# A graph attention layer on one core: the second half of the one-hots turned at the first tile of a group

## The reference

```python
def head(w1, bb1, w2, bb2, a1, aab1, a2, aab2):
    feats = jnp.maximum(x @ w1 + bb1, 0.0) @ w2 + bb2
    x_cat = jnp.concatenate([feats[row], feats[col], elem[:, None]], axis=1)
    hid = jnp.maximum(x_cat @ a1 + aab1, 0.0)
    e1 = (hid @ a2 + aab2)[:, 0]
    e1 = jax.nn.leaky_relu(e1, negative_slope=0.2)
    w = jnp.exp(e1 - jnp.max(e1))
    pooled = jax.ops.segment_sum(w[:, None] * feats[col], row, num_segments=n)
    row_sum = jax.ops.segment_sum(w, row, num_segments=n) + 1e-10
    return pooled / row_sum[:, None]
...
x = _layernorm(x + _L0_gnn_ref(x, edge_index, edge_weight, ...), axis=-1)
```

## Time and profile before

| | us |
|---|---|
| median of 3 timed runs | 5230.21 (5229.04 to 5233.76) |
| the profiled execution | 5190.44 |
| its span, first to last instruction | 5188.7 |
| tile loop | about 1700 to 4960 |
| busy, share of the span | PE 85%, DVE 88%, ACT 72%, POOL 52% |
| granted TensorE clock, mean | 0.956 |

### The profile page before, as it was taken

How to read it: one execution, slowest core, us unless ns; L and a number is a source line. 1 busy time by engine, 2 the same in 40 slices (tenths; PEclk the granted TensorE clock), 3 DMA queues, 4 the chain that set the end, 5 groups by cost and what they waited for, 6 DMA issues and landing times.

```text
span 5188.7 us, 133139 instructions
## 1 busy us (share of the span) xinstructions
PE 4402.2 (85%) x24914; PEld 3093.9 (60%) x24915; DVE 4550.7 (88%) x25629; ACT 3761.1 (72%) x12720; POOL 2702.7 (52%) x2834
## 2 busy tenths in 40 slices
PE   1499899999986899999999999999999999999920
PEld 0255555555554666767677767767677767767610
DVE  7799999999998789888899889889898889898853
ACT  0467766766762688888888888888888888888832
POOL 1266666666666555555555555555555555555522
PEclk9799999999997999999999999999999999999965
DMA  2032333333333777777777777777777777777623
GB/s 79 23 73 67 78 72 71 75 74 72 69 78 93 227 216 218 218 219 217 216 218 217 217 218 219 217 218 216 217 218 216 219 215 219 215 220 216 200 87 117
DMA packets 287022, 850.50 MB, mean 164 GB/s; under 512 B 98946, under 2 KB 138114, under 8 KB 286966
## 3 DMA queue, kind: packets, MB, share of 16 engines
q0 software_dynamic: 169920, 673.54, 46.8%
q1 hardware_dynamic: 74638, 160.14, 9.7%
q10 hardware_dynamic: 42408, 16.21, 1.2%
HBM read 738.46 MB, written 111.26 MB: 164 GB/s over the span
## 4 chain that ended last, share of the span: by engine, by line
PE 29%; ACT 25%; DVE 6%; issue 4%; DMA 4%; DVEq 1%; POOL 0%; ACTq 0%; POOLq 0%; SPq 0%
ACT z L1092 17%; PE psum L949 12%; PE psum L953 7%; PE psum L936 6%; DVE z L1503 3%; ACT onehot L1121 3%; DMA out_dram<-z 3%; ACT onehot_t L1110 3%; PE psum L962 2%; ACT onehot L1125 2%; PE psum L973 1%; DVE z L1493 1%; PE psum L921 1%; DVE acc L1552 1%; DVEq L1552 0%
## 5 line engine op out<-in xcount | busy, mean ns | idle before, releaser
L734 POOL DMA_INDIRECT z<-qf_table,rec x1664 | 1593.6, 958 | 1567.0 <-PE psum L936 1035.8
L1092 ACT ACTIVATE z<-z 128x64 f32<-128x64 f32 x6656 | 1651.5, 336 | 56.6 <-ACT z L1099 56.3
L949 PE MATMUL psum<-p_win,onehot_t 128*128 x9984 | 1434.0, 276 | 207.7 <-ACT onehot_t L1110 90.5
L949 PEld LDWEIGHTS psum<-p_win,onehot_t 128*128 128x128 bf16 x9984 | 963.9, 97 | 777.8 <-issue 460.6
L936 PE MATMUL psum<-z,onehot 128*128 128x260 f32 x3328 | 1027.2, 391 | 2.8 <-DVE acc L1552 1.9
L953 PE MATMUL psum<-z,ident 128*128 128x258 f32 x3328 | 1004.0, 383 | 0.0
L1503 DVE SCALAR_TENSOR_TENSOR z<-z,a_b 128x129 f32<-128x129 f32 x3328 | 893.0, 292 | 0.0
L1503 DVE SCALAR_TENSOR_TENSOR z<-psum,a_b 128x129 f32<-128x129 f32 x3328 | 822.6, 283 | 0.0
L1552 DVE TENSOR_TENSOR acc<-acc,psum 125x260 f32 x1664 | 698.7, 420 | 78.6 <-PE psum L936 48.8
L1493 DVE TENSOR_TENSOR z<-z,psum 128x258 f32<-128x258 f32 x1664 | 691.9, 416 | 39.4 <-PE psum L953 29.6
L666 POOL DMA_INDIRECT sorted_rows<-z x300 | 483.3, 1611 | 406.9 <-DVE z L1384 162.4
(11 more groups left out here) (221 smaller groups left out, 6363.0 us busy)
## 6 DMA issues: line engine op xcount, KB each, us to landing
p_table<-acc SPq DMA_DIRECT2D x100, 377.9 KB
p_win<-p_table SPq DMA_DIRECT2D x100, 377.9 KB
qf_table<-acc SPq DMA_DIRECT2D x75, 378.9 KB
z<-qf_table,rec POOLq DMA_INDIRECT x1664, 4.6
acc<-in_x_dram SPq DMA_DIRECT2D x25, 500.0 KB
z<-in_x_dram SPq DMA_DIRECT2D x20, 625.0 KB
out_dram<-z ACTq DMA_DIRECT2D x20, 625.0 KB
qf_table<-z SPq DMA_DIRECT2D x25, 378.9 KB
```

The source lines that it names most:

```text
L734: pool.indirect_dma_start(out=z_t[:, o + j, :], out_offset=None, in_=qf_table, in_offset=bass.IndirectOffsetOnAxis(ap=rec[:, o + j, 3:4].b ...
L949: mm = pe.matmul(to, onehot_t[:, j, :], p_flat[:, bass.ds((w % 2) * (3 * ZW) + (part * ZW + o), n)], start=(part == 0), stop=(part == 2 an ...
L1092: op = act.activation(z_t[:, slot, o:o + DO], z_t[:, slot, o:o + DO], ACT.Copy, scale=z_t[:, slot, o + DO:o + HF])
```

## The change

The turn of the second half of a group's one-hots moves on TensorE from behind the third `hidden_src` to behind the first. The copy of this half on ScalarE moves from the head of the group's own step to the step before, between the weights of the sixth and the seventh tile. Nothing is computed otherwise.

```diff
                 for j in range(SB):
                     if live(i, k, 0):
                         hidden_src(j)
-                    if j == SB // 4 and live(i, k, 0):
+                    if j == 0 and live(i, k, 0):
                         turn(0, 1)
                     if j == SB // 4 and live(i, k, -1):
                         max_t()
...
-                if live(i, k, 0):
-                    take_turned(0, 1)
                 if live(i, k, 1):
                     onehots(1, 0)
                 if live(i, k, -1):
...
                     if j == SB // 2 and live(i, k, 1):
                         onehots(1, 1)
+                    if j == SB - 3 and live(i, k, 1):
+                        take_turned(1, 1)
```

## The result

The changed kernel took 6033.2 us (median of 4 runs, 6031.1 to 6048.4) beside 5230.3 for the kernel before: 1.154 times as long, 95% interval 1.152 to 1.156. The forecast was 6231 us with a range of 5570 to 6330. The profiled execution took 6033.65 us, 843 more than that of before.

The account below looks back on a forecast made before the run. VectorE was taken to bound the loop; 17.33 us per group plus 3.1 for the clock gave 20.43 against 15.57, over 206 groups 1001 us, plus 5190.4 profiled and 39.8 offset: 6231 us, range 5570 to 6330.

Parts of the forecast that it names:

- part 1: TensorE, at the moved turn: it waits 2.3 to 3.0 us per group for the second half's one-hots.
- parts 2 and 3: VectorE's delay behind the turn and the closed cycle: 8.19 + 2.38 + 6.70, corrected to 17.33 us per group against 15.57.
- T: End of ScalarE's Relu for the second half's one-hots, put at 8.19 us after `e_sh`.
- part 5: TensorE's clock in the loop: the stall halves it in nearly every group, costing 3.1 us each.
- rival B: Clock in the loop: falls for only 3.4 us or in some groups; 5881 us, mixtures 5700 to 6100; chance 0.22.
- main case: Whole loop: stall plus 6.8 us at half clock, 20.43 us per group; 6231 us (6130 to 6330); chance 0.43.
- the sort's row: Trace of the sort: clock fell inside a TensorE pause, 6.8 us at half; taken as model for the loop.
- the tail: Trace's end: after a 1.73 us pause and smaller ones the clock fell for 3.4 us, TensorE working from its start.
- VectorE bounds the loop, and the copy's wait is worth 0.3 us at most: Tile loop before: VectorE limits it; removing all its waits for TensorE would bring 0.2 to 0.3 us per group.
- part 4: ScalarE's moved copy: waits for nothing, own time neither saved nor added; `onehots(1, 0)` starts at about T + 5.9.
- D: Moved turn: its one-hots are ready when it is reached; 5168 us at best, 5230 without gain; chance 0.07.
- A: Loop: only the stall costs, clock stays at 2.4 GHz; 5593 us (5525 to 5670); chance 0.22.

Follow-up runs that it names:

- turn_only: The kernel before with only TensorE's turn moved to behind the first hidden_src, the copy left in place: 6022.7 us, 1.160 times before.
- oh_third: The changed kernel with ScalarE's onehots(1, 1) moved from behind the fifth weight to behind the third: 5271.2 us, 1.008 times before.
- oh_second: The changed kernel with ScalarE's onehots(1, 1) moved from behind the fifth weight to behind the second: 5145.3 us, 0.984 times before.
- fill8: The changed kernel with 8 needless f32 products on constants on TensorE ahead of the turn: 5609.2 us, 1.073 times before.
- copy_only: The changed kernel with the turn back behind the third hidden_src, so only ScalarE's copy moves: 5045.8 us, 0.9725 times before.
- extra_before: The kernel before with two needless small copies on ScalarE ahead of the second half's copy at the step's head: 5248.9 us, 1.0116 times before.
- turn_at_1: The changed kernel with the turn behind the second hidden_src instead of the first: 5252.7 us, 1.012 times before.
- split_dve: copy_only with the second of VectorE's two register loads moved from the group's start to ahead of the fourth tile: 5048.8 us, 0.9729 times before.

## Why the prediction was right, and where it was off

*The stall* (part 1): forecast 2.3 to 3.0 us ahead of the turn, measured 2.84. *Right*, forecast from the trace of before alone; `turn_only` shows that it needs nothing else, `oh_third` and `oh_second` that it hangs on the time of the one-hots and not on the place as such.

*The cycle* (parts 2 and 3): forecast 17.33 us a group at full clock, measured 17.35 to 17.47 in the groups without a fall and 17.41 as a typical value in `fill8`. The terms hold too, by the medians of the eight groups without a fall: from T to the second tile forecast 2.38, measured 2.41; from there to `e_sh` forecast 6.70, measured 6.75. ScalarE's part, forecast 8.19, measured 8.25 in the group shown. *Right.*

*The clock falls* (part 5): forecast in nearly every group. The clock fell in 165 of 173 groups. *Right*, and `fill8` shows that idleness of TensorE is what brings it: with 1.0 us of pause on average the clock fell in 2 of 136 groups. The length of the pause alone doesn't decide: eight groups with the full pause of 2.4 to 3.1 us had no fall, and `oh_third` has falls at shorter ones. The page of the Trainium skill named in the prediction (TensorE: Matmul & The Clock Gate, HAM oscillation) would have it stay up here; the trace does not agree.

*What the fall costs*: this is the term that was mis-sized. I put 3.1 us on every group, for 6.8 us at the low level, and gave the short fall (3.4 us, a loss of 1.4) as rival B. Both occur, half and half. In the long groups T to the exponentials took 12.06 us (3503.36 to 3515.42), where the sum has 9.1 without a fall, a loss of 2.9. In the short ones it took 10.5 where the clock fell inside the stall, a loss of 1.4, and 10.9 where it fell behind it, 1.7. The groups take 20.2 to 20.4 and 18.7 to 19.2 us, where main case and B have 20.43 and 18.73. The two prices were about right and the share was wrong: 2.15 us on average instead of 3.1. My reason for taking the sort's row was that the low level would begin inside the pause. It began behind the pause in 42 of the 165 falls, as in the tail, and in 43 more it began inside and was short all the same. By its own ranges the forecast's main case (6130 to 6330) missed; 6033 us lies in rival B's mixtures (5700 to 6100), and the stated range holds it because it was drawn wide enough to take in both. That the two lengths came out even is nothing that the prediction knew, and why a fall takes one or the other is open beyond the times named above.

*Medians*: I added 39.8 us because the timed runs of before lay that much above its profile. The changed kernel's median is that of its profile (6033.2 and 6033.7). The difference of the profiles, 843 us, is 158 less than my 1001, that of the medians 198; the offset should have gone into the range. Of the 158, the groups account for more than all, 206 x (20.43 - 19.56) = 179 us; the rest of the kernel came out 21 us longer than in the profile of before, and 179 - 21 + 40 are the 198. Most of that lies ahead of the loop: the first exponentials start at 1752 us against 1728, and so they do, within 6 us, in all four runs on the chip where before takes 5230 us. They start at 1728 in `turn_only`, so it isn't the edit.

*VectorE bounds the loop, and the copy's wait is worth 0.3 us at most*: *wrong*, though it changed nothing in the result. I read it from the list of waits, where VectorE's for TensorE came to 0.21 us. `copy_only` gained 0.70. It holds for `copy_only` at most. The kernel before was held by the cycle through ScalarE and the copy (part 4 has it that the copy's own time is "neither saved nor added"), as `extra_before` shows: 0.29 us added ahead of the copy, 0.29 us more a group. The list shows each engine's waits and not that they close into one cycle, and it left out small ones: all of VectorE's idle time beyond its loads came to 0.49 us a group, not 0.21. In `copy_only` VectorE's instructions also got 0.23 us a group shorter, which no list of waits could tell.

*The copy waits for nothing* (part 4): at half clock it waited 0.33 us for the turn, inside ScalarE's slack. `onehots(1, 0)` started at T + 8.8 in the long group instead of T + 5.9, since TensorE was slow; `e_sh` still came 1.23 us behind its end. Harmless, as said.

*Not slower* (D) and *only the stall* (A) are ruled out by the profile after: no group is shorter than 17.35 us, and the clock is 0.88.

## What to carry to other kernels

Before a step with a wait is moved forward in an engine's queue, find when its input is ready against the new place, and follow the cycle that closes through the other engines: the wait came back here in each of the 174 groups of the stretch because the input itself hangs on the stalled engine. A pause of some microseconds on TensorE may cost as much again by its clock, and useless products in the pause win that half back; moving the input forward wins both. When a change has two halves, time each alone: here one lost 16% and hid that the other gains 2.75%. And before the result of an added delay is read, measure the delay in the trace: here two copies taken for 0.48 us were 0.29, and only with that number do they show that the whole path counts.

## What the runs showed of the hardware

With pauses of TensorE of 2.4 to 3.1 us (a few up to 4.0) that recur every 17 to 20 us, and TensorE busy between them, the granted clock fell to the lower level (1.2 GHz) in 165 of 173 groups of the changed kernel and in all of `turn_only`, most often inside the pause, in a quarter of the groups about 1.1 us behind it with TensorE at work. Pauses of up to 1.3 us (`fill8`) and 1.55 us (`turn_at_1`) that recur in the same way left it up, but nine falls came at single pauses of 0.6 to 2.2 us in `oh_third` and two at 2.2 us in `fill8`. It was then held for 3.4 or 6.8 us: in the changed kernel the longer in all 80 falls that came 0.72 us or more ahead of the end of the pause, the shorter in the 85 that came later. At the low level the four transposes have a pitch of 0.91 us in all against 0.43, the two f32 products of the sum 0.86 against 0.44. VectorE's instructions of one form took 1 to 3% less in `copy_only` than in before, but hardly in `split_dve`, which is as fast; the cause is open. Two ScalarE copies of 128x64 with a duration of 0.24 us each follow one another at a pitch of 0.146 us and push the next instruction back by 0.29 us, less than their durations add up to; the weights' instructions, of the same size, follow one another at 0.24 us.
